# Sparse part of layer two with the expert's weights as the stationary side, from a ring of four copies

## The reference, cut to what matters

```python
logits = xt @ router_w.T
topk_vals, topk_idx = jax.lax.top_k(logits, 2)
g = jax.nn.sigmoid(topk_vals)
g = g / (g.sum(axis=-1, keepdims=True) + 1e-10)
for e in range(8):
    ge = jnp.sum(jnp.where(topk_idx == e, g, 0), axis=-1)
    h = jax.nn.silu(xt @ w_gate[e]) * (xt @ w_up[e])
    out = out + ge[:, None] * (h @ w_down[e])
```

## Time and profile before

| what | us |
|---|---|
| median of three runs | 356.2 |
| the runs | 356.11, 356.20, 359.04 |
| profiled execution, its own time | 354.63 |
| its span, first to last instruction | 352.6 |
| TensorE busy in the span | 309.5 |
| VectorE busy | 238.7 |
| GpSimd busy | 213.3 |
| ScalarE busy | 177.1 |
| mean granted TensorE clock | 0.938 of full |

### The profile page before, as it was taken

How to read it: one execution, slowest core, us unless ns; L and a number is a source line. 1 busy time by engine, 2 the same in 40 slices (tenths; PEclk the granted TensorE clock), 3 DMA queues, 4 the chain that set the end, 5 groups by cost and what they waited for, 6 DMA issues and landing times.

```text
span 352.6 us, 6882 instructions
## 1 busy us (share of the span) xinstructions
PE 309.5 (88%) x1825; PEld 239.1 (68%) x1825; DVE 238.7 (68%) x902; ACT 177.1 (50%) x495; POOL 213.3 (60%) x252
## 2 busy tenths in 40 slices
PE   8889978899999999999888769769899999999800
PEld 3789957688988898888777644445466766676500
DVE  4987924788888888888988835994964542323206
ACT  2936766666665565556566420641512146656500
POOL 8899963557778877866775441337772015565620
PEclk9958999999999999999999958976999999999975
DMA  7960326027778855543355006001111202222144
GB/s 225 307 217 1 121 92 257 16 92 272 271 257 298 292 195 177 170 158 132 106 190 182 32 23 238 2 0 52 53 54 44 57 23 74 77 86 68 47 150 170
DMA packets 27382, 46.55 MB, mean 132 GB/s; under 512 B 4305, under 2 KB 15377, under 8 KB 27217
## 3 DMA queue, kind: packets, MB, share of 16 engines
q1 hardware_dynamic: 17360, 28.45, 23.1%
q0 software_dynamic: 4256, 8.74, 7.8%
q10 hardware_dynamic: 5728, 8.93, 7.2%
HBM read 15.90 MB, written 14.87 MB: 87 GB/s over the span
## 4 chain that ended last, share of the span: by engine, by line
PE 59%; DVE 21%; issue 7%; DMA 5%; POOL 5%; ACT 1%; SPq 0%; POOLq 0%; DVEq 0%; ACTq 0%
PE psum L1067 13%; PE psum L1155 6%; PE psum L1087 5%; POOL yrows L679 5%; DVE x L1535 4%; PE psum L1114 4%; PE psum L1124 4%; PE psum L1211 4%; PE psum L1092 4%; PE psum L1167 3%; PE psum L1108 3%; DMA blocks<-yrows 2%; DVE bn L1259 2%; DVE blocks L507 2%; PE psum L990 2%
## 5 line engine op out<-in xcount | busy, mean ns | idle before, releaser
L679 POOL DMA_INDIRECT yrows<-yx,sid x31 | 29.6, 955 | 40.4 <-ACT yx L888 38.1
L648 POOL TENSOR_TENSOR rh<-c2ve,neghalf 128x8 f32<-128x8 f32 (+1 forms) x23 | 34.1, 1482 | 29.1 <-DVE c2ve L1511 29.0
L634 POOL DMA_INDIRECT yrows<-yx,sidx x39 | 39.4, 1010 | 11.7 <-issue 9.0
L623 POOL DMA_INDIRECT xg<-xrows,gidx x39 | 38.3, 983 | 13.1 <-issue 11.3
L1067 PE MATMUL psum<-yx,blocks 128*128 128x256 f32 (+1 forms) x184 | 43.2, 358 | 1.2 <-DMA blocks<-rec 1.2
L1563 DVE TENSOR_TENSOR x1T<-psum,xn 128x256 f32<-128x256 f32 x31 | 13.2, 425 | 33.1 <-ACT xn L882 33.0
L1155 PE MATMUL psum<-x1T,rec 128*128 128x512 f32 x64 | 33.4, 659 | 1.6 <-DVE wraw L1548 1.6
L1211 PE MATMUL psum<-rec,yx 128*128 x62 | 31.8, 595 | 0.0
L1067 PEld LDWEIGHTS psum<-yx,blocks 128*128 128x128 f32 x184 | 29.3, 191 | 3.1 <-ACT yx L829 1.4
L804 ACT ACTIVATE x1T<-psum 128x512 f32<-128x512 f32 (+1 forms) x23 | 12.3, 533 | 36.0 <-PE psum L1092 31.7
L1535 DVE SCALAR_TENSOR_TENSOR x<-blocks,wh,x 128x128 f32<-128x128 f32 x56 | 16.1, 353 | 18.8 <-DMA blocks<-yrows 18.5
(11 more groups left out here) (259 smaller groups left out, 806.4 us busy)
## 6 DMA issues: line engine op xcount, KB each, us to landing
blocks<-rec SPq DMA_DIRECT2D x23, 523.0 KB
xslots<-frow ACTq DMA_DIRECT2D x6, 1032.0 KB
blocks<-yrows SPq DMA_DIRECT2D x7, 512.0 KB, 5.2
blocks<-wd SPq DMA_DIRECT2D x23, 128.0 KB
wraw<-in_L_attn_w_up SPq DMA_DIRECT2D x4, 512.0 KB, 7.1
blocks<-xslots SPq DMA_DIRECT2D x31, 64.5 KB, 1.9
x<-in_L_attn_hidden_states SPq DMA_DIRECT2D x4, 256.0 KB, 4.5
rec<-in_L_ffn_w_gate SPq DMA_DIRECT2D x1, 1024.0 KB, 11.0
```

The costliest lines, as they stand in the source:

```text
L623: g.indirect_dma_start(xg[:, b, h, :], None, xrows, bass.IndirectOffsetOnAxis(ap=gidx[0][:, unit(j) + h:unit(j) + h + 1], axis=0)).then_in ...
L634: g.indirect_dma_start(yrows[0], bass.IndirectOffsetOnAxis(ap=sidx[0][:, unit(j) + h:unit(j) + h + 1], axis=0), yx[:, (j + 2) % RY, 0, h * ...
L648: g.tensor_tensor(rh[:, 0:n], c2ve[:, 0:n], neghalf[:, 0:n * NH].rearrange("p (h k) -> p h k", h=n), ALU.pow).then_inc(s_rh, 1)
L679: g.indirect_dma_start(yrows[1], bass.IndirectOffsetOnAxis(ap=sid[:, j:j + 1], axis=0), yb2[:, j % R2Y, :], None).then_inc(s_scat2[j % R2Y ...
```

## The change

The gate/up product of a sparse tile is turned round: the weights are stationary, four pieces of 128 columns, and `xT2` moves 128 tokens past each. `GU2` then has channels in the partitions, 128 tokens for each of four chunks, so `hh2` comes out as down wants it, without a transpose. TensorE's transposes of `hh2`, their bank, ScalarE's copy to `hT2` and the two semaphores go, and down and its copy follow one step sooner.

The stationary side is read from `w2buf`, a ring of R2W = 4 copies of 512 columns (256 KB over the 128 partitions) in the unused `ypair` area. SP loads copy j from `rec2` with a register that it loads from the tile map; from tile 4 on it waits that gate/up of the tile four earlier is done. Loads of slots and of weights go through SP in the order written: weights 0 to 3, the wait for the dispatch, slots 0 to 7, and then slots j+4 and weights j in turn for j = 4 to 30. Down still takes its weights from `rec2` as the moving side.

```diff
+R2W = 4
+        w2buf = ypair[:, 0:R2W * 2 * I // D, :].rearrange("p m d -> p (m d)").rearrange("p (b n) -> p b n", b=R2W)
-        hT2 = xg[:].rearrange("p b h d -> p (b h d)").rearrange("p (b t) -> p b t", t=I)
...
 SP:
-            sp.wait_ge(s_disp, 16 * TOPK * (TT - DN))
             sp.wait_ge(s_late, 64)
             sp.wait_ge(s_exp[1], 1)
-            for j in range(N2):
+
+            def load_gate_up(j):
+
+                at_least(sp, s_g, j - R2W + 1)
+                e = sp.value_load(expert[1][0:1, j:j + 1], min_val=0, max_val=E - 1)
+                sp.dma_start(w2buf[:, j % R2W, :], rec2[:, bass.ds(e, 1), GATE:GATE + 2 * I].rearrange("p a n -> p (a n)"))\
+                    .then_inc(s_w2[j % R2W], 16)
+
+            def load_slots(j):
+
+                if j >= N2:
+                    return
                 if j >= R2I:
                     sp.wait_ge(s_xtp[1], j - R2I + 1)
                     sp.wait_ge(s_scat2[(j - R2I) % R2Y], 16 * ((j - R2I) // R2Y + 1))
                 at = sp.value_load(rowt[0:1, j:j + 1], min_val=0, max_val=EMPTY)
                 sp.dma_start(xin2[:, j % R2I, :], ...).then_inc(s_in2[j % R2I], 16)
+
+            for j in range(R2W):
+                load_gate_up(j)
+            sp.wait_ge(s_disp, 16 * TOPK * (TT - DN))
+            for j in range(8):
+                load_slots(j)
+            for j in range(R2W, N2):
+                load_slots(j + 4)
+                load_gate_up(j)
...
 ScalarE, loop2:
-                if 0 <= s - 2 < N2:
-                    j = s - 2
-                    act.wait_ge(s_htp, j + 1)
-                    at_least(act, s_y[1], j - R2H + 1)
-                    a.activation(hT2[:, j % R2H, :], HT2, ACT.Copy).then_inc(s_hts, 1)
...
-                if 0 <= s - 3 < N2:
-                    j = s - 3
+                if 0 <= s - 2 < N2:
+                    j = s - 2
                     act.wait_ge(s_y[1], j + 1)
...
 TensorE, loop2:
-                    t.matmul(GU2[s % R2G], xT2[:, s % R2Y, :],
-                             rec2[:, bass.ds(expert_of[s], 1), GATE:GATE + 2 * I].rearrange("p a n -> p (a n)"),
-                             start=True, stop=True).then_inc(s_g, 1)
+                    pe.wait_ge(s_w2[s % R2W], 16 * (s // R2W + 1))
+                    for c in range(2 * CH):
+                        ins = t.matmul(GU2[s % R2G][:, c * P:(c + 1) * P], w2buf[:, s % R2W, c * P:(c + 1) * P], xT2[:, s % R2Y, :], start=True, stop=True)
+                    ins.then_inc(s_g, 1)
...
                     pe.wait_ge(s_hh, j + 1)
-                    at_least(pe, s_hts, j)
-                    for c in range(CH):
-                        ins = t.transpose(HT2[:, c * P:(c + 1) * P], hh2[:, j % R2H, c * P:(c + 1) * P], ident[:])
-                    ins.then_inc(s_htp, 1)
-                if 0 <= s - 3 < N2:
-                    j = s - 3
-                    pe.wait_ge(s_hts, j + 1)
                     at_least(pe, s_yb, j)
...
-                        ins = t.matmul(Y2, hT2[:, j % R2H, c * P:(c + 1) * P],
+                        ins = t.matmul(Y2, hh2[:, j % R2H, c * P:(c + 1) * P],
...
 VectorE, tile_hidden:
-                at_least(dve, s_htp, j - R2H + 1)
+                at_least(dve, s_y[1], j - R2H + 1)
```

More of the change, by code:

```diff
@@ L305, in program @@
             "ca_ready", "prod_ready", "zz_ready", "vs_ready", "h1_ready", "hs_ready"))
-        s_g, s_thg, s_hh, s_htp, s_hts = (sem(n) for n in (
-            "gate_up_psum", "silu_gate", "ffn_h", "hT_psum", "hT_copied"))
+        s_w2 = [sem(f"gate_up_in{b}") for b in range(R2W)]
+        s_g, s_thg, s_hh = (sem(n) for n in ("gate_up_psum", "silu_gate", "ffn_h"))
         s_fid, s_fill, s_slot, s_id1 = (sem(n) for n in ("fill_ids_ready", "slots_filled", "slots_ready", "pair_ids_ready"))
@@ L333, in program @@
         Yd = [bank[b][:, :].rearrange("p (i d) -> p i d", d=D) for b in (4, 7)]
-        XT2, GU2, HT2, Y2 = bank[0][:, 0:P], [bank[b][:, :] for b in (1, 2)], bank[3][:, 0:I], bank[4][:, 0:D]
+        XT2, GU2, Y2 = bank[0][:, 0:P], [bank[b][:, :] for b in (1, 2)], bank[4][:, 0:D]
         block = ctx.enter_context(nc.Block())
```

## The result

The changed kernel takes 366.19 us (median of 4 runs, 365.85 to 372.31), the kernel before 357.62 in the same measurement; the ratio is 1.0236 with a 95% interval of 1.0162 to 1.0311. It is slower in both: the medians stand 8.6 and 10.9 apart. The forecast was 367.0, slower with 0.90.

What follows compares the result with a forecast made beforehand. TensorE bound the kernel before; SP's queue would bind after. Last gate/up 12.3 us later, less 1.5 of tail, gives +10.8 on the 356.2 median: 367.0 us, range 361.5 to 377.

Steps and rivals of the forecast that it cites:

- The bound before: Sparse tiles before the change: TensorE busy all of 287 to 330 us, one step of 1.64 us per tile.
- TensorE's part: Sparse tiles: TensorE's step falls from 1.64 to 1.45 us; alone this would gain 6.1 us in all.
- SP's pace: SP's queue in sparse tiles: slot load plus weight copy take 2.42 us a tile and become the bound.
- The count: SP's loads followed through the sparse tiles: last gate/up starts at 342.6 instead of 330.32, +12.3 us.
- The tail: Last gate/up to last scatter: 4.72 us instead of 6.18, a gain of 1.5 us.
- The 20 pairs: SP's slot and weight loads from load 6 to 26: 2.42 us each, from 286.1 to 334.5.
- The gap: SP's queue: 0.34 us with nothing visible once every twelve loads, counted as 0.06 a tile.
- B: SP's queue, with register loads stretched by the copies' traffic: 2.80 us a tile, 374.6 us; chance 0.13.
- C: TensorE's clock falls in the new gaps: step 2.90 us at half clock, about 377 us; chance 0.11.
- D: SP's preparation overlaps or is short, so SP holds 1.45 a tile; TensorE stays the bound, 350.1 us; chance 0.06.
- E: The ring's round trip through gate/up or scatter binds: 1.4 to 1.7 us a tile, 350 to 357; chance 0.04.
- A: The forecast itself: SP's queue sets the pace, 2.2 to 2.6 us a tile, 361 to 371 us; chance 0.66.

Runs made afterwards that it cites:

- e5: Changed kernel without copies or waits for them; TensorE reads resident weights of an expert named in the program text: 346.15 us, ratio 0.9811 to the kernel before.
- e9: Changed kernel with each copy's register load, its arithmetic and check done twice: 383.63 us, ratio 1.0779 to the kernel before.
- e1: Changed kernel with each copy's expert taken from the program text instead of a loaded register: 358.49 us, ratio 1.0141 to the kernel before.
- e4: Changed kernel with SP loading registers of four tiles by one instruction, without range check: 354.31 us, ratio 0.9994 to the kernel before.
- e10: Changed kernel with slot loads of tiles 12 to 30 issued by ScalarE instead of SP: 356.18 us, ratio 1.0073 to the kernel before.
- e2: Changed kernel with each copy moving only the gate columns, 128 KB instead of 256 KB: 369.12 us, ratio 1.0442 to the kernel before.
- e3: Kernel before with SP's 31 weight copies added and nobody reading them: 367.36 us, ratio 1.0378 to the kernel before.
- e8: Changed kernel measured again as it is: 366.18 us, ratio 1.0375 to the kernel before.
- e6: Changed kernel with registers of four tiles by one load and a ring of eight copies: 349.43 us, ratio 0.9851 to the kernel before.

## Why the prediction was right

**The bound before and TensorE's part.** The step of 1.45 was measured twice, in e5 and as the eight records and their neighbours after the change. The 6.1 us it would bring alone were 6.2 in the sparse part of e5 and 1.9%, some 6.7, in the time.

**SP's pace.** The decisive term, 2.42 a tile from 1.10 + 1.21 + 0.05 + 0.06, measured 2.40 to 2.41 in most pairs, with two at 2.76 and 2.74 and one at 2.52. It came from rows of two different stages, added because one in-order queue issues both. e9 (add register load: slower), e1 and e4 (take it away: faster), e10 (another queue: faster), e2 (half the bytes: no gain) and e3 (the loads without their use: as slow) all point to this one term.

**The count.** Last slot load's partner, copy 26, at 333.93 (worked out 334.5), copy 30 at 338.8 (339.4), landing 2.3 (2.44), last gate/up 342.28 (342.6). The tail was 4.64 (4.72). That the span fits within 0.4 rests in part on luck, because errors of either sign cancel. Copies 4 and 5 were to wait for gate/up 0 and 1, but these ran at 277.98 and 280.70 instead of 279.41 and 282.10 (the part ahead of them was quicker in this execution), SP's waits for them came to 0.2, and copy 6 went out at 284.99 instead of 286.1: 1.1 less. The 20 pairs from there took 2.45 on average instead of 2.42, 0.5 more. The gap was not the reason: it came twice in these 40 loads, less often than the once in twelve that one sample had given. The quiet pair was 2.40 to 2.41, where the sum has 2.36 without the gap, and a single register load of 0.40 made the 2.52. The last four steps, from gate/up 26 at 336.41, took 5.87 instead of 5.6, the first of them 1.74. The median's agreement (366.19 for 367.0) rests on its base as well: the forecast adds 10.8 to 356.2, the medians of this measurement stand 8.6 apart on a base of 357.62, those of e8's 10.9 on 355.31.

**The rivals.** B fell: the register loads of the changed kernel kept a median of 0.273, 0.396 at most. (The long one in the saturated stretch of the earlier trace rows took 0.947; the 0.977 quoted for it is the longest of the line, at another time.) They do stretch where loads stand closer: in e4 single ones took up to 1.33. C did not decide the changed kernel (clock 1.00 in the tiles), but its mechanism is real: in e2 and e3 the clock fell after one longer wait. It stayed at 1.00 through the regular gaps of some 0.9 and through a single one of 1.52 (ahead of the gate/up at 305.17); after waits of 3.1 (e2) and of 1.6 with a thin stretch ahead of it (e3) it stood near half. D fell as worked out, and with it, for this case, what the Trainium skill says ("DMA: Bandwidth & Descriptors", Issuing engines are not separate DMA queues), that initiating a DMA is usually small beside the DMA itself: 1.21 of issue a copy bounded the kernel while its 2.3 of flight did not. E was underrated as a second limit. It doesn't bind at 2.4, but in e1 and e4, with SP's pair at 1.67 and 1.28, it took a good part of what SP gave back: their sparse parts are 57.0 and 55.8, where TensorE alone needs 50.9 (e5). I had put 0.04 on it for this kernel, which is fair, but in the expectations of e1 and e4 I should have counted it. The range was to begin at A's lower end, which is 361 by its own figures; it was given from 361.5.

## What to carry to other kernels

Price a load that is added per tile by what its issue holds in the queue that issues it: register load, arithmetic, check, waits and the DMA instruction, here 1.1 to 1.2 us a load with 64.5, 128 and 256 KB alike, and add it to all that the same queue issues per tile. A queue that shows no busy time in the page can become the bound; compare its sum with the step of the busiest engine before you give that engine less to do. If such loads are needed, fetch the registers of several tiles at once, and give the ring a lead longer than the landing under load.

## What the runs showed of the hardware that was not expected

- One register load can fill four registers; with that and without the range check, SP's pair of loads fell from 2.41 to 1.28 (e4). What each of the two gave was not measured apart.
- The landing of a 256 KB copy inside the chip's buffers was 2.3 as a median with the DMA engines half busy (after, e8), 3.0 (e4, where they were 0.59 to 0.66 busy from 280 to 320) and 3.5 (e6, 0.64 to 0.75 busy from 300 to 320), with single ones near 4.
- TensorE's granted clock stayed 1.00 with TensorE 70% busy in short gaps and one of 1.52 after the change, and was about half (0.53, 0.50) after one gap of 3.1 in e2 and one of 1.6 for slot rows in e3.
- A DMA instruction of a copy, 0.47 (e1) and 0.49 (e4) as a median, held SP's queue for up to 1.38 (e1) and 1.34 (e4) where the copies stood closer. Why is open; in the changed kernel the longest was 0.51.
